# Turning the attention results inside the fourth head's slot, dividing before its last maximum, splitting the maxima on GpSimd, and batch 2's last sum later

## The chip, the cores and the metric

The kernel runs on one core of one Trainium2 chip. The time is that of one execution in device microseconds; the kernel before took 545.0 us, the median of three executions (544.27 to 546.27). TensorE (PE in the rows) multiplies and writes PSUM, which has eight banks of 128x512 float32; VectorE (DVE) and ScalarE (ACT) read PSUM; GpSimd (POOL) works on SBUF only; SyncE (SP) issues DMAs. Each engine runs its own stream in order, and streams wait for one another by semaphores.

## The reference

Four sequences of 512 rows with 128 channels go through two blocks, each with a normalization before and after. `H` is 16 heads.

```python
x = x + layernorm(attention1(layernorm(x)))        # 16 heads of 8, rotary, causal
x = x + layernorm(ffn_block(layernorm(x)))

def attention(...):                                 # both blocks, per head
    scores = q @ k.T * scale                        # 512 x 512
    scores = where(causal, scores, -big)
    attn = softmax(scores)                          # exp(s - max) / sum
    return (attn @ v) @ Wo

def ffn_block(x):
    x = x + attention2(rmsnorm(x, w_ln1))           # 16 heads of 64, keys and values from a latent of 16
    y = rmsnorm(x, w_ln2)
    return x + mean(shared_experts(y)) + sum(top2_gate(y) * experts(y))
```

## The kernel before

**Groups and slots.** The 16 heads of a sequence are taken four at a time. There are 32 such groups (`NG`), 16 of the first block's attention (`LAYER` 1) and then 16 of the second's (`LAYER` 2). The program of every engine is written out slot by slot: in slot n, `stream` runs `main(n, hh)` for the four heads `hh` and behind each head the stages that the table `beside()` puts there (norms, projections, rotations, experts of other sequences). Three groups are in work in one slot:

- group n+2: scores for the row maxima (`scores_for_max`, L574/L576, with the causal mask added by L601), 11 bank fills per slot. VectorE reads each fill and leaves the negated maxima in `NM` (`maximum`, L1263 and L1273). The last fill of a slot, (head 3, i 3), holds the first 128 rows of four heads.
- group n: scores for the exponentials (`scores_for_exp`, L610/L616), ten units per slot; ScalarE's L895 turns each into probabilities in `PG`. The bank of a unit comes free when the exponential three units back is done. The row maximum enters these scores as additional rows of the queries.
- group n-1: GpSimd zeroes what lies above the diagonal in four blocks (L1209 or L1216, semaphore `causal`); TensorE multiplies with the values in four steps j (`values`, L659), all into the one bank `BK_O`; ScalarE copies that bank to `OT` (L901, `ot_ready`); TensorE turns it back into the same bank (`turn_out`, L666, `o_turned`).

**Who waits around the change.** In the kernel before, `turn_out(n-1)` is the last thing of head 3 on TensorE. VectorE divides by the sums (`divide`: reciprocal L1311 into `rec`, product L1320 into `ON1`, or into `ON2`, which the rows call `room`, since it lies in `room1`; semaphore `on_ready`) in the next slot, between the first maxima of head 0. The first `values` step of the next group sits behind head 1's first two units and waits for `on_ready`, for `causal` and for `exp_done`. Probabilities lie in two halves of `PG`.

**The split of the maxima.** The maxima go to TensorE's operands in parts of lower precision: for block 1 three bfloat16 parts (`MB`; four VectorE steps L1293 to L1299), for block 2 two parts (`MF`; two steps L1301 and L1303), each step waiting for the one before (`m_step`). In slot n, VectorE splits group n+1 between the maxima of head 0. TensorE turns the parts at the end of head 1 (`turnmax`, L707/L710), ScalarE copies them to `MP` and SyncE's DMA writes them into the query rows, for slot n+1.

**The end.** Behind the last group, slot 33 holds what is left of sequences 2 and 3. VectorE takes the stages of that list in its order: `o2y` of sequence 3 (sum and variance), `y3` of sequence 2 (L1617, then the statistics), `rms2` of sequence 3 (L1494: tiles 2 and 3 of `xn`; ScalarE scales tiles 0 and 1), then `logit`, the routing and the experts.

Of the kernel before, what the change touches and what calls it, by code (L numbers as in the profile page):

```python
# [16 lines left out]
F32 = mybir.dt.float32  # L17
# [51 lines left out]
def beside():  # L69
# [17 lines left out]
    def experts(b, n, slots):  # L87
# [54 lines left out]
        ("y3", 2, 0), ("rms2", 3, 0), ("x3T", 3, 0), ("logit", 3, 0))]  # L142
# [116 lines left out]
def block_program(nc, x, wqkv, wo1, wkva, wq_nope, wq_rope, wkvb, wo2, ln1w, ln2w, wgate, gbias, wgu, wgu_s, wd,  # L259
                  wd_s, ident, masks, rope1, ropek, ropeq, rank, expert_rows, out):  # L260
    with ExitStack() as ctx:
# [298 lines left out]
        def _(pe):  # L560
# [116 lines left out]
            def main(n, hh):  # L677

                if hh == 0 and n + 2 < NG:
                    m = n + 2  # L680
                    if m == 0:
                        pe.wait_ge(consts_ready, CONSTS)

                if n + 2 == 0 and hh == 2:
                    pe.wait_ge(stack1_late, 32)
                for i in range(4):
                    if 0 <= n < NG and i < 2 + hh % 2:
                        scores_for_exp(n, hh, i)
                    if n + 2 < NG and i < fills_of(hh)[1]:
                        if hh == 0 and i == 0:  # L690
                            stack_loaded(n + 2)
                        scores_for_max(n + 2, hh, i)
                    if 1 <= n <= NG and (hh, i) in VALUES_AT:
                        values(n - 1, VALUES_AT.index((hh, i)))
                if hh == 3 and 1 <= n <= NG:
                    turn_out(n - 1)
# [401 lines left out]
        def _(pool):  # L1098
# [103 lines left out]
            def causal_blocks1(n):  # L1202
# [3 lines left out]
                for j in CAUSAL_ORDER:  # L1206
# [11 lines left out]

            def main(n, hh):
                if hh == 0 and 1 <= n <= NG and LAYER[n - 1] == 1:  # L1220
                    causal_blocks1(n - 1)
                if hh == 2 and 0 <= n < NG and LAYER[n] == 2:
                    causal_blocks2(n)
# [12 lines left out]
        def _(dve):  # L1236
# [45 lines left out]
            def split_max(n, i):  # L1282

                m = NM[:, :, HG * (n % G):HG * (n % G) + HG]
                if i == 0:
                    dve.wait_ge(fill_read, (n + 1) * FILLS)
                    if n:
                        dve.wait_ge(bank_full, BANK0["turnmax", n - 1, 0] + 1)
                elif MSTEPS[n] + i < MSTEPS[n + 1]:
                    dve.wait_ge(m_step, MSTEPS[n] + i)  # L1290
                if LAYER[n] == 1:
                    if i == 0:
                        dve.tensor_copy(MB[:, :, 0, :], m).then_inc(m_step, 1)  # L1293
                    elif i == 1:
                        dve.tensor_tensor(MRest[:], m, MB[:, :, 0, :], ALU.subtract).then_inc(m_step, 1)
                    elif i == 2:
                        dve.tensor_copy(MB[:, :, 1, :], MRest[:]).then_inc(m_step, 1)
                    else:
                        dve.tensor_tensor(MB[:, :, 2, :], MRest[:], MB[:, :, 1, :], ALU.subtract).then_inc(m_step, 1)  # L1299
                elif i == 0:  # L1300
                    dve.tensor_copy(MF[:, :, 0, :], m).then_inc(m_step, 1)  # L1301
                elif i == 1:
                    dve.tensor_tensor(MF[:, :, 1, :], m, MF[:, :, 0, :].bitcast(F32), ALU.subtract).then_inc(m_step, 1)  # L1303
# [20 lines left out]
            def main(n, hh):  # L1324
                split, out = hh == 0 and 0 < n + 1 < NG, hh == 0 and 2 <= n <= NG + 1
                if hh == 0 and n == -1:
                    for i in range(4):
                        split_max(0, i)
                for i in range(4):
                    if split:  # L1330
                        split_max(n + 1, i)
                    if out and i < 2:
                        divide(n - 2, i)
# [371 lines left out]
```

## Time and profile before

| | |
|---|---|
| median of three executions | 545.0 us (544.27 to 546.27) |
| profiled execution, whole time | 546.34 us |
| its span, first to last instruction | 544.6 us |
| mean granted TensorE clock | 0.983 of full speed |
| TensorE matmul busy | 491.0 us, 90% of the span |
| VectorE busy | 401.6 us, 74% |
| ScalarE busy | 312.4 us, 57% |
| GpSimd busy | 200.6 us, 37% |

Durations below come from the one profiled execution. A matmul's row spans its latency, so matmuls in a row overlap. "Idle before" in square brackets is the time in which the engine did nothing ahead of the row, with what ended it; for an instruction that waits for several engines, this name is only an inference. A GpSimd row's span is rough.

### The profile page before, as it was taken

Reading aid. Unit: us, or ns where it says so; the run is one execution under the profiler, and the core shown is the slowest. Engines: PE = TensorE matmul, PEld = TensorE weight load, DVE = VectorE, ACT = ScalarE, POOL = GpSimd, SP = SyncE. Lnnn points to the kernel's source line nnn. Section 1 sums busy time; section 2 is a strip of 40 time slices with the busy share of each in tenths; the row PEclk is TensorE's granted clock in tenths of the full one; section 3 lists DMA queues with packets and bytes.
Section 4 is the critical chain, followed back from the end, with each engine's and each line's share of the span. In section 5 each row is a group of like instructions: output and inputs, shape, how many; then the busy total and the mean of one; then the engine's idle time right before and its main releaser. Section 6 shows DMA issues by size and latency. Waiting matters only on the chain.

```text
span 544.6 us, 9510 instructions
## 1 busy us (share of the span) xinstructions
PE 491.0 (90%) x3190; PEld 281.9 (52%) x3190; DVE 401.6 (74%) x1209; ACT 312.4 (57%) x586; POOL 200.6 (37%) x268
## 2 busy tenths in 40 slices
PE   7788989988799889989999999998989898898784
PEld 3443444434354345556565666564856474554643
DVE  6789998799489977975786687775676854464475
ACT  1586785767667785666756546544465433654230
POOL 5522663365236642664346514521041100510100
PEclk9999999989999999999999999999999998999988
DMA  6455533114223634548345652632303200000000
GB/s 147 132 159 182 159 114 118 45 47 143 82 85 123 172 68 107 107 123 156 117 105 110 125 136 86 135 58 58 59 21 61 58 2 2 20 2 0 2 13 26
DMA packets 29673, 47.17 MB, mean 87 GB/s; under 512 B 4649, under 2 KB 15145, under 8 KB 29113
## 3 DMA queue, kind: packets, MB, share of 16 engines
q1 hardware_dynamic: 28496, 45.72, 32.5%
q10 hardware_dynamic: 1128, 0.85, 0.7%
q8 instruction: 25, 0.41, 0.4%
q14 instruction: 24, 0.19, 0.1%
HBM read 27.22 MB, written 18.87 MB: 85 GB/s over the span
## 4 chain that ended last, share of the span: by engine, by line
PE 58%; DVE 15%; ACT 14%; issue 5%; POOL 4%; DMA 2%; SPq 1%; ACTq 1%; DVEq 0%; POOLq 0%
PE ps L659 14%; PE ps L616 11%; PE ps L729 10%; PE ps L576 5%; DVE ps L1273 4%; ACT PG L895 4%; PE ps L610 4%; PE ps L862 3%; PE ps L574 2%; ACT xn L1034 2%; PE ps L780 2%; PE ps L710 2%; PE ps L601 1%; ACT QS L970 1%; DMA rope_sb<-in_rope 1%
## 5 line engine op out<-in xcount | busy, mean ns | idle before, releaser
L895 ACT ACTIVATE PG<-ps 128x512 f32<-128x512 f32 x320 | 178.5, 600 | 127.6 <-PE ps L616 81.9
L1273 DVE CUSTOM_DVE_ANT_0 ps<-ps,below 128x512 f32<-128x512 f32 (+1 forms) x256 | 156.1, 638 | 40.9 <-PE ps L576 21.8
L616 PE MATMUL ps<-QS,K 128*128 128x512 f32 x320 | 115.8, 446 | 4.8 <-ACT PG L895 3.1
L659 PE MATMUL ps<-PG,V 128*32 128x512 f32 (+3 forms) x1024 | 97.1, 452 | 12.2 <-DVE ON L1320 5.1
L616 PEld LDWEIGHTS ps<-QS,K 128*128 128x128 f32 x320 | 54.0, 190 | 47.7 <-ACT PG L895 21.4
L1263 DVE TENSOR_REDUCE NM<-ps 128x2 f32<-128x512 f32 (+1 forms) x96 | 63.3, 685 | 16.3 <-PE ps L601 16.1
L576 PE MATMUL ps<-K,QS 96*128 96x256 f32 (+3 forms) x256 | 71.4, 336 | 1.1 <-DVEq L1589 0.9
L610 PE MATMUL ps<-QS,KS 128*128 128x128 bf16 (+3 forms) x256 | 62.0, 303 | 5.6 <-ACT PG L895 3.0
L574 PE MATMUL ps<-KS,QS 96*128 96x256 bf16 (+3 forms) x256 | 63.3, 300 | 0.5 <-DVE terms L1379 0.4
L1108 POOL TENSOR_TENSOR rstd<-ve,half 128x4 f32<-128x4 f32 x20 | 20.3, 1017 | 111.8 <-DVE ve L1255 77.9
L1216 POOL TENSOR_SCALAR_AFFINE_SELECT PG<-PG 128x512 f32<-128x512 f32 x64 | 39.7, 643 | 50.0 <-ACT PG L895 49.6
L1209 POOL TENSOR_SCALAR_AFFINE_SELECT PG<-PG 128x512 f32<-128x512 f32 x64 | 38.6, 635 | 41.7 <-ACT PG L895 41.7
L1164 POOL TENSOR_TENSOR whole<-terms 128x512 f32<-128x512 f32 x27 | 34.2, 1277 | 53.3 <-DVE terms L1379 32.4
L576 PEld LDWEIGHTS ps<-K,QS 96*128 96x128 f32 x256 | 44.5, 190 | 10.9 <-DVEq L1589 1.4
L659 PEld LDWEIGHTS ps<-PG,V 128*32 128x32 f32 x1024 | 21.0, 108 | 52.5 <-issue 36.3
L610 PEld LDWEIGHTS ps<-QS,KS 128*128 128x128 bf16 x256 | 19.4, 98 | 49.0 <-ACT PG L895 27.7
L729 PE MATMUL ps<-QS,KS 128*128 128x512 f32 x72 | 35.9, 622 | 0.0
L1273 DVE DVE_READ_ACCUMULATOR2_ANT NM<- 128x1 f32 x256 | 35.8, 140 | 0.0
L601 PE MATMUL ps<-below,identb 128*128 128x256 bf16 (+1 forms) x96 | 30.2, 315 | 0.0
L574 PEld LDWEIGHTS ps<-KS,QS 96*128 96x128 bf16 x256 | 23.2, 97 | 13.2 <-DVE NM L1273 2.8
L1197 POOL TENSOR_TENSOR QC<-whole,QC 128x512 fp32r<-128x512 f32 x16 | 20.5, 1280 | 21.7 <-ACT QC L1017 21.5
L564 PE MATMUL ps<-OT 128*128 128x512 bf16 x76 | 23.7, 424 | 1.5 <-DVE two_ones L1625 1.5
(170 smaller groups left out, 676.5 us busy)
## 6 DMA issues: line engine op xcount, KB each, us to landing
scr<-QC SPq DMA_DIRECT2D x24, 512.0 KB, 2.8
QS<-scr SPq DMA_DIRECT2D x64, 128.0 KB
scr<-room SPq DMA_DIRECT2D x20, 256.0 KB, 2.6
QS<-scr SPq DMA_DIRECT2D x15, 288.0 KB
KS<-scr SPq DMA_DIRECT2D x15, 288.0 KB
QS<-scr SPq DMA_DIRECT2D x64, 64.0 KB
x<-in_x SPq DMA_DIRECT2D x4, 256.0 KB, 3.3
out_x<-x SPq DMA_DIRECT2D x3, 256.0 KB, 2.3
```

Of the source, the lines that this page charges most:

```text
L574: return pe.matmul(dst, QS1[0:MROW, h, P * i:P * i + P], KS1[0:MROW, h, 0:P * k], start=first, stop=alone, skip_group_check=not alone)
L576: return pe.matmul(dst, QS2[0:MROW, h, P * i:P * i + P], K1[0:MROW, SEQ[n] % 2, 0:P * k], start=first, stop=alone, skip_group_check=not alone)
L601: mm = pe.matmul(last, identb[:], below[:, 3 * P:T].unsqueeze(1).to_broadcast([P, heads, P]), start=False, stop=True, skip_group_check=True)
L610: return pe.matmul(dst, KS1[:, h, q0:q0 + P], QS1[:, h, q0:T], start=True, stop=True)
L616: mm = pe.matmul(bank.rearrange("p (h q) -> p h q", h=HG), keys[:, SEQ[n] % 2, P * j:P * j + P], QS2[:, heads, P * i:P * i + P], start=(ke ...
L659: mm = pe.matmul(out, v, p, start=(j == 0), stop=(j == NT - 1), skip_group_check=True)
L729: pe.matmul(bank(u)[0:rows, :], w, xT, start=True, stop=True).then_inc(bank_full, 1)
L895: act.activation(PG[:, n % 2, unit_place(LAYER[n], (u + k) % UNITS), :], ps[:, BANK_OF["unit", u + k], :], ACT.Exp, scale=scale).then_inc( ...
L1209: pool.affine_select(blocks, blocks, pattern=[*heads, [1, P]], compare_op=ALU.is_ge, fill=0.0, base=0, channel_multiplier=-1).then_inc(cau ...
L1216: pool.affine_select(blocks, blocks, pattern=[[0, HG], [1, P]], compare_op=ALU.is_ge, fill=0.0, base=0, channel_multiplier=-1).then_inc(ca ...
L1263: dve.tensor_reduce(dst, src, AX.X, ALU.max, negate=True).then_inc(fill_read, 1)
L1273: dve.tensor_tensor_reduce(out=bank[:, 0:w], in0=bank[:, 0:w], in1=below[:, T - w:T], scale=-1.0, scalar=-NEG, op0=ALU.add, op1=ALU.min, a ...
```

## The change

Four edits:

1. `turn_out(n-1)` is issued in the middle of head 3: behind its second pair (exponential unit and maximum fill, i = 1), ahead of unit i = 2 and the fills i = 2 and 3.
2. `divide(n-1)` moves from head 0 of the next slot to head 3 of the same slot, both instructions together, ahead of the last maximum (i = 3).
3. The splits of groups 1 to 31 move from VectorE to GpSimd, at head 0. In block 1's slots they stand between the second and the third of the four causal blocks; group 0's stays on VectorE. GpSimd's split waits for all maxima of its group (`fill_read`) and for the turn of the previous group's parts.
4. In slot 33's list `rms2` of sequence 3 is ahead of `y3` of sequence 2.

```diff
-        ("y3", 2, 0), ("rms2", 3, 0), ("x3T", 3, 0), ("logit", 3, 0))]
+        ("rms2", 3, 0), ("y3", 2, 0), ("x3T", 3, 0), ("logit", 3, 0))]
...
                     if 1 <= n <= NG and (hh, i) in VALUES_AT:
                         values(n - 1, VALUES_AT.index((hh, i)))
-                if hh == 3 and 1 <= n <= NG:
-                    turn_out(n - 1)
+                    if 1 <= n <= NG and (hh, i) == (3, 1):
+                        turn_out(n - 1)
...
+            def split_max(n):
+                m, done = NM[:, :, HG * (n % G):HG * (n % G) + HG], MSTEPS[n]
+                pool.wait_ge(fill_read, (n + 1) * FILLS)
+                pool.wait_ge(bank_full, BANK0["turnmax", n - 1, 0] + 1)
+                if LAYER[n] == 1:
+                    pool.tensor_copy(MB[:, :, 0, :], m).then_inc(m_step, 1)
+                    pool.wait_ge(m_step, done + 1)
+                    pool.tensor_tensor(MRest[:], m, MB[:, :, 0, :], ALU.subtract).then_inc(m_step, 1)
...
+                masked1 = hh == 0 and 1 <= n <= NG and LAYER[n - 1] == 1
+                if masked1:
+                    causal_blocks1(n - 1, CAUSAL_ORDER[:2])
+                if hh == 0 and n >= 0 and n + 1 < NG:
+                    split_max(n + 1)
+                if masked1:
+                    causal_blocks1(n - 1, CAUSAL_ORDER[2:])
...
-                split, out = hh == 0 and 0 < n + 1 < NG, hh == 0 and 2 <= n <= NG + 1
+                out = hh == 3 and 1 <= n <= NG
                 if hh == 0 and n == -1:
-                    for i in range(4):
-                        split_max(0, i)
+                    split_max0()
                 for i in range(4):
-                    if split:
-                        split_max(n + 1, i)
-                    if out and i < 2:
-                        divide(n - 2, i)
+                    if out and i == 3:
+                        divide(n - 1, 0)
+                        divide(n - 1, 1)
                     if n + 2 < NG and i < 2 + hh % 2 + hh // 3:
                         maximum(n + 2, hh, i)
```

TensorE, the end of a slot of block 1 before: L610 is the third exponential unit of head 3, L574 with L601 the two last fills, L666 the turn of the results.

```order
L574 MATMUL ps<-KS,QS 128x384 [waits fill_read]
L610 MATMUL ps<-QS,KS 128x256 [waits exp_done]
L610 MATMUL ps<-QS,KS 128x256
L574 MATMUL ps<-KS,QS 128x256 [waits fill_read]
L574 MATMUL ps<-KS,QS 128x256
L601 MATMUL ps<-below,identb 128x2x128
L574 MATMUL ps<-KS,QS 128x128 [waits fill_read]
L574 MATMUL ps<-KS,QS 128x128 x3
L601 MATMUL ps<-below,identb 128x512
L666 MATMUL ps<-ident_sb,OT 128x128 [waits ot_ready]
L666 MATMUL ps<-ident_sb,OT 128x128 x3
```

The same place now:

```order
L574 MATMUL ps<-KS,QS 128x384 [waits fill_read]
L666 MATMUL ps<-ident_sb,OT 128x128 [waits ot_ready]
L666 MATMUL ps<-ident_sb,OT 128x128 x3
L610 MATMUL ps<-QS,KS 128x256 [waits exp_done]
L610 MATMUL ps<-QS,KS 128x256
L574 MATMUL ps<-KS,QS 128x256 [waits fill_read]
L574 MATMUL ps<-KS,QS 128x256
L601 MATMUL ps<-below,identb 128x2x128
L574 MATMUL ps<-KS,QS 128x128 [waits fill_read]
L574 MATMUL ps<-KS,QS 128x128 x3
L601 MATMUL ps<-below,identb 128x512
```

The four matmuls of the turn, with their wait for ScalarE's copy, have moved ahead of ten others.

VectorE from the two last fills of a slot on, before (L1263 reads a fill of several heads, L1273 one head's, L1311 and L1320 divide):

```order
L1263 TENSOR_REDUCE NM<-ps 128x2 [waits score_fill]
L1263 TENSOR_REDUCE NM<-ps 128x4 [waits score_fill]
L1293 CAST MB<-NM 128x4x4 [waits bank_full,fill_read]
L1311 RECIPROCAL rec<-ps 128x16 [waits o_turned]
L1273 ISA ps,NM<-ps,below 128x512 [waits score_fill]
L1273 ISA NM 128x1
L1295 TENSOR_TENSOR MRest<-NM,MB 128x16 [waits m_step]
L1320 TENSOR_TENSOR ON<-ps,rec 128x4x32 [waits rec_ready]
L1273 ISA ps,NM<-ps,below 128x384 [waits score_fill]
```

The same place now (the lines are numbered anew: L1286 and L1296 are the maxima, L1323 and L1332 the division):

```order
L1286 TENSOR_REDUCE NM<-ps 128x2 [waits score_fill]
L1323 RECIPROCAL rec<-ps 128x16 [waits o_turned]
L1332 TENSOR_TENSOR ON<-ps,rec 128x4x32 [waits rec_ready]
L1286 TENSOR_REDUCE NM<-ps 128x4 [waits score_fill]
L1296 ISA ps,NM<-ps,below 128x512 [waits score_fill]
L1296 ISA NM 128x1
L1296 ISA ps,NM<-ps,below 128x384 [waits score_fill]
```

The division stands one fill earlier than it did, and no split is left in the row. On GpSimd, four causal blocks of a slot stood in a row before:

```order
L1209 AFFINE_SELECT PG<-PG 128x4x128 [waits exp_done,cleared]
L1209 AFFINE_SELECT PG<-PG 128x4x128 x3
L1164 TENSOR_TENSOR whole<-terms 128x512 [waits terms_ready] x2
```

Now the split (L1225 to L1231) is among them:

```order
L1209 AFFINE_SELECT PG<-PG 128x4x128 [waits exp_done,cleared]
L1209 AFFINE_SELECT PG<-PG 128x4x128
L1225 CAST MB<-NM 128x4x4 [waits bank_full,fill_read]
L1227 TENSOR_TENSOR MRest<-NM,MB 128x16 [waits m_step]
L1229 CAST MB<-MRest 128x4x4 [waits m_step]
L1231 TENSOR_TENSOR MB<-MRest,MB 128x4x4 [waits m_step]
L1209 AFFINE_SELECT PG<-PG 128x4x128 [waits exp_done]
L1209 AFFINE_SELECT PG<-PG 128x4x128
```

The third and fourth blocks, and what GpSimd has behind them, come after the split's four steps.

## Rows read from the trace of the kernel before

**Rows 1.** Waits of PE: engine, line, released by: us in total, times, longest us
```profile
PE ps L659 <- DVE ON L1320: 5.1, 5, 1.3
PE ps L659 <- DVE room L1320: 4.6, 4, 1.9
PE ps L724 <- ACT PG L895: 3.4, 4, 1.0
...
PE ps L610 <- ACT PG L895: 3.0, 6, 0.9
...
PE ps L659 <- ACT PG L895: 1.4, 3, 0.5
...
PE ps L659 <- POOL PG L1216: 1.1, 2, 0.8
```

**Rows 2.** Timeline of PE, end of one slot of block 1: start us, us
```profile
78.49 0.38 PE L610 MATMUL ps<-QS,KS 128*128 128x256 bf16 x2
...
79.49 0.60 PE L666 MATMUL ps<-ident_sb,OT 128*128 128x128 f32 x4
...
82.56 1.07 PE L659 MATMUL ps<-PG,V 128*32 128x512 f32 x8 [1.22 <-DVE ON L1320]
```

**Rows 3.** Timeline of DVE, one split step at the slot's start
```profile
70.28 0.88 DVE L1293 CAST MB<-NM 128x16 bf16<-128x16 f32 x1
```

**Rows 4.** Timeline of POOL, the same time and one slot later
```profile
68.86 2.27 POOL L1174 TENSOR_TENSOR terms<-whole,room 128x512 f32<-128x512 f32 x2 [3.03 <-ACT room L935]
71.08 2.41 POOL L1209 TENSOR_SCALAR_AFFINE_SELECT PG<-PG 128x512 f32<-128x512 f32 x4
...
80.36 2.41 POOL L1209 TENSOR_SCALAR_AFFINE_SELECT PG<-PG 128x512 f32<-128x512 f32 x4 [4.41 <-ACT PG L895]
```

**Rows 5.** Timeline of ACT, the copy ahead of the turn, in block 1 and block 2
```profile
78.22 0.60 ACT L901 ACTIVATE OT<-ps 128x512 f32<-128x512 f32 x1
...
346.96 0.60 ACT L901 ACTIVATE OT<-ps 128x512 f32<-128x512 f32 x1
```

**Rows 6.** Timeline of PE, the third unit of head 3 in block 2
```profile
348.55 0.63 PE L616 MATMUL ps<-QS,K 128*128 128x512 f32 x2
```

**Rows 7.** Groups of POOL by form: busy us, mean ns of one
```profile
L1108 POOL TENSOR_TENSOR rstd<-ve,half 128x4 f32<-128x4 f32 x20 | 20.3, 1017 | 111.8 <-DVE ve L1255 77.9 <-DVE ve L1521 22.1 <-DVE ve L1529 11.4
...
L1118 POOL TENSOR_TENSOR nmean<-nmean,rstd 128x4 f32<-128x4 f32 x16 | 3.2, 199 | 1.3
```

**Rows 8.** Groups of DVE by form: first and last of the six split steps
```profile
L1293 DVE CAST MB<-NM 128x16 bf16<-128x16 f32 x16 | 6.3, 394 | 0.5
...
L1301 DVE CAST MF<-NM 128x16 fp32r<-128x16 f32 x16 | 4.7, 296 | 0.8 <-DVE QS L1602 0.2 <-DVE CT L1569 0.2
```

**Rows 9.** Timeline of PE, a turn of the maxima's parts
```profile
76.06 0.39 PE L707 MATMUL ps<-identb,MB 128*12 128x128 bf16 x4
```

**Rows 10.** Window: us; PE, PEld, DVE, ACT, POOL busy; granted clock; DMA; GB/s
```profile
116.60:120.00 3.40, 3.35 (x15) 0.71 (x19) 3.30 (x14) 1.22 (x3) 3.14 (x4) 0.50 0.07 17
```

**Rows 11.** Timeline of PE where the clock falls, and in slot 32
```profile
116.65 1.94 PE L659 MATMUL ps<-PG,V 128*32 128x512 f32 x8 [1.26 <-DVE ON L1320]
...
454.56 1.93 PE L659 MATMUL ps<-PG,V 128*32 128x512 f32 x8 [1.85 <-DVE room L1320]
...
500.96 2.14 PE L659 MATMUL ps<-PG,V 128*32 128x512 f32 x24 [1.87 <-DVE room L1320]
```

**Rows 12.** Timeline of DVE in slot 33
```profile
513.17 0.69 DVE L1617 TENSOR_TENSOR KS<-room,ps 128x512 f32<-128x512 f32 x1 [0.88 <-PE ps L862]
...
515.37 0.47 DVE L1494 TENSOR_SCALAR xn<-KS,rstd 128x128 f32<-128x128 f32 x2
519.25 0.19 DVE L1537 TENSOR_TENSOR KS<-ps,gbias_sb 128x32 f32<-128x32 f32 x1 [3.42 <-PE ps L825]
```

**Rows 13.** Timeline of POOL, then of PE, in slot 33
```profile
512.38 1.01 POOL L1108 TENSOR_TENSOR rstd<-ve,half 128x4 f32<-128x4 f32 x1 [22.12 <-DVE ve L1521]
...
515.89 0.67 PE L724 MATMUL ps<-ident_sb,xn 128*128 128x128 f32 x2 [1.24 <-DVE xn L1494]
```

More of the change, by code:

```diff
@@ L1200, in ropeB, with causal_blocks1 @@
                 pool.sem_inc(job_done[j], 1)
-            def causal_blocks1(n):
+            def causal_blocks1(n, order):
                 pair = PG[:, n % 2, 0:8, :].rearrange("p (h k) t -> p h k t", k=2)
@@ L1205, in causal_blocks1 @@
                 pool.wait_ge(exp_done, UNITS * (n + 1))
-                for j in CAUSAL_ORDER:
+                for j in order:
                     blocks = (pair[:, :, 0, 0:P], pair[:, :, 1, 0:P], both[:, :, :, 0:P], pair[:, :, 1, 3 * P:T])[j]
@@ L1217, in causal_blocks2 @@
                                        channel_multiplier=-1).then_inc(causal, 1)
-            def main(n, hh):
-                if hh == 0 and 1 <= n <= NG and LAYER[n - 1] == 1:
-                    causal_blocks1(n - 1)
+            def split_max(n):
[6 more added lines that the diff above has]
+                    pool.tensor_tensor(MRest[:], m, MB[:, :, 0, :], ALU.subtract).then_inc(m_step, 1)
+                    pool.wait_ge(m_step, done + 2)
+                    pool.tensor_copy(MB[:, :, 1, :], MRest[:]).then_inc(m_step, 1)
+                    pool.wait_ge(m_step, done + 3)
+                    pool.tensor_tensor(MB[:, :, 2, :], MRest[:], MB[:, :, 1, :], ALU.subtract).then_inc(m_step, 1)
+                else:
+                    pool.tensor_copy(MF[:, :, 0, :], m).then_inc(m_step, 1)
+                    pool.wait_ge(m_step, done + 1)
+                    pool.tensor_tensor(MF[:, :, 1, :], m, MF[:, :, 0, :].bitcast(F32), ALU.subtract).then_inc(m_step, 1)
+            def main(n, hh):
+                masked1 = hh == 0 and 1 <= n <= NG and LAYER[n - 1] == 1
[5 more added lines that the diff above has]
+                    causal_blocks1(n - 1, CAUSAL_ORDER[2:])
                 if hh == 2 and 0 <= n < NG and LAYER[n] == 2:
@@ L1280, in maximum, with split_max0 @@
                 reduce_fill(n, k, src, dst)
[L1282 to L1303, printed above, removed]
+            def split_max0():
+                m = NM[:, :, 0:HG]
+                dve.wait_ge(fill_read, FILLS)
+                dve.tensor_copy(MB[:, :, 0, :], m).then_inc(m_step, 1)
+                dve.wait_ge(m_step, 1)
+                dve.tensor_tensor(MRest[:], m, MB[:, :, 0, :], ALU.subtract).then_inc(m_step, 1)
+                dve.wait_ge(m_step, 2)
+                dve.tensor_copy(MB[:, :, 1, :], MRest[:]).then_inc(m_step, 1)
+                dve.wait_ge(m_step, 3)
+                dve.tensor_tensor(MB[:, :, 2, :], MRest[:], MB[:, :, 1, :], ALU.subtract).then_inc(m_step, 1)
             def divide(n, i):
```

## The prediction
> **What bounds the kernel.** I read first who waits for whom on each engine, then the timelines of single slots, then the windows with the granted clock. TensorE is the engine to follow: its matmuls cover nine tenths of the span, and ScalarE and GpSimd idle often. So a change is worth what it takes from TensorE's waits or adds to them. The longest of these in the middle of the program stand ahead of the first values step of a slot, for VectorE's division: 5.1 us in five places and 4.6 us in four, 9.7 us together [rows 1]. The other large one is for an exponential bank at a slot's end (3.4 us ahead of L724, 3.0 ahead of L610) [rows 1]; the change doesn't address that.
>
> **The division (edits 1 and 2).** In the slot shown, the turn L666 ran at 79.49 us and the next values step started at 82.56, after 1.22 us of waiting [rows 2]: in between VectorE had two maxima to finish, a split step, another maximum, and only then the product. Now both instructions come right behind the turn and ahead of a maximum, at least one maximum before the old place, and the values step lies some ten matmuls behind the turn. I take it that no values step waits for the division any more. What is late next is the first causal block. In the slot shown GpSimd starts its four at 80.36 and needs 2.41 us for all [rows 4], a quarter of it is 0.60, so the first is done at 80.96, before TensorE comes. In the slot ahead, GpSimd is held up by L1174 and starts them at 71.08 [rows 4]; the first is done at 71.68, while TensorE's preceding matmul ends about 71.4. There 0.3 us of the wait stays. I count two such slots: 9.7 - 0.6 = 9.1 us. Five more waits ahead of L659 carry another name, 1.4 us in three places (ScalarE) and 1.1 in two (GpSimd) [rows 1]; in most of them the division was in fact the last to end, and I count 1.0 us of the 2.5. Sum: 10.1 us less. Bounds: 9.7 + 2.5 = 12.2 at most, and 1.9 at least (the wait of slot 32 alone, 1.87 us [rows 11], where no exponentials follow that could take its place).
>
> **The turn's own wait (edit 1).** The turn waits for ScalarE's copy. In block 1 that copy ends at 78.22 + 0.60 = 78.82 [rows 5], and TensorE reaches the new place, where L610 starts now, at 78.49 [rows 2]: it will stand 0.33 us, with some 0.06 us for the signal 0.4. The copy follows the exponential of head 2, which itself follows TensorE, so this distance repeats from slot to slot; I find it at 0.33 to 0.43 us in thirteen of block 1's sixteen slots. In eight of these TensorE waits right behind the turn for ScalarE anyway (the waits of L610 and L724 in [rows 1]), and standing earlier costs nothing there. Five are left: 5 x 0.4 = 2.0 us, and 0.3 for a slot or two more. In block 2 the copy ends at 346.96 + 0.60 = 347.56 and TensorE arrives at 348.55 [rows 5, 6], 1 us later: no wait. Cost 2.3 us; bounds 0 and 14 x 0.4 = 5.6. On ScalarE the third exponential of head 3 comes after two others of 0.6 us each behind the copy, which is about the time that the turn takes on TensorE, so it is not late. VectorE's last maximum comes 0.6 us later, but the next slot starts without the split.
>
> **The split (edit 3).** The six step groups of VectorE took 33.0 us in all (6.3 the first and 4.7 the last listed [rows 8]), all but the first group's go. The mean of 394 ns hides two kinds: 0.17 us when alone, 0.88 us at 70.28 [rows 3], ending with GpSimd's L1174 at 71.13 [rows 4]. VectorE isn't the bound, so I value the 32 us at nothing beyond the division's earlier place; bounds 0 and 2 us less (waits of TensorE for routing and rotations, which VectorE's other work delays).
>
> What it costs is four steps in GpSimd's row between causal blocks 2 and 3. The trace has none of this shape there; between 199 ns for a product of 128x4 and 1017 ns for a power of 128x4 [rows 7], I take 0.2 us and 0.07 for each step's signal, nearest to the product, since copies and subtractions are like it: 4 x 0.27 = 1.1 us in block 1, 0.5 in block 2. In the slot shown the split then runs 81.6 to 82.7 and the third block ends at 83.3; its values step comes 2.9 us behind the first, near 84.2 even when this starts 1.2 us sooner. The turn of the parts is later still: at 76.06 [rows 9] in a slot whose split would end at 73.4. So both are covered by 0.9 us and more, and in block 2, where the causal blocks aren't behind the split, by over 2 us. Value nothing; bounds 0 and the rival below.
>
> The Trainium skill (SBUF — State Buffer, "SBUF: two separate sides") says that VectorE and GpSimd share a port pair as an exclusive lock, taken by a GpSimd instruction or by a VectorE one with two SBUF inputs; the trace agrees with the 0.88 us step. By this rule the four steps can in turn be held by such a VectorE instruction, some 0.7 us each time, which would use up most of the cover but not change the sum. The skill (GPSIMD Engine Reference, "Engine selection") advises VectorE for elementwise work and gives GpSimd about half the speed with two inputs. At 0.17 us here that would be 0.35 a step, 1.6 us for four, still under the cover; no row here shows this shape.
>
> **The clock.** From 116.60 to 120.00 the granted clock is 0.50, TensorE's lower level of 1.2 GHz, while PE is busy 3.35 of 3.40 us [rows 10]; the same holds from 454.5 to 457.9. Both begin within 0.1 us of the end of a long wait for the division, 1.26 and 1.85 us [rows 11], and the eight matmuls there took 1.94 and 1.93 instead of 1.07 us [rows 2, 11]. Other waits of 1.2 us didn't lower it, so this is no law. If those two go, each gives back 0.9 us for the matmuls and some 0.3 for the next: 2.4 us less. Bounds: 3.4 less (half of both windows), and 3.4 more if as much low clock appears elsewhere.
>
> **The end (edit 4).** VectorE runs L1617 from 513.17 with its statistics until L1494 can start at 515.37 [rows 12]; the scale that L1494 needs is there from 512.38 + 1.01 = 513.39 on [rows 13]. Moved ahead it ends near 514.0, and TensorE's second pair of turns, which waited 1.24 us for it [rows 13], follows the first without a wait. Gain 1.2 us. The 2.2 us of L1617 and statistics then lie from 514.0 to 516.3, ahead of L1537, which would start near 518.0 (519.25 less 1.2) [rows 12]; GpSimd's scale and the store of sequence 2 have 20 us left. Bounds 0.8 and 1.3.
>
> **Sum.** 10.1 + 1.2 + 2.4 less, 2.3 more: 11.4 us. I let 0.9 go in one slot in which ScalarE waits for a chain over GpSimd (the norm of sequence 1 or 0) and not for TensorE: 10.5 us. The profiled execution took 546.34 us with a span of 544.6; it becomes 535.8 with a span of 534.1. The median shown is 1.3 us below that execution, so the forecast is 545.0 - 10.5 = 534.5 us. What a measurement tells from no change is 0.5%, 2.7 us.
>
> **Rivals.**
> *The turn's wait is paid in full.* If the slots lose their bank wait once TensorE runs sooner, all fourteen pay 0.4 us, 5.6 in all, and stretches of low clock stay: 10.1 + 1.2 - 5.6 = 5.7 less, 539.3 us. For it speaks the constancy of the 0.33 us; against it that the bank waits come from ScalarE's own work in those slots.
> *The clock falls elsewhere.* Four new stretches like [rows 10] cost 1.7 us each, 6.8, and the two old ones stay in part: 545.0 - 10.5 + 6.8 = 541.3 us. For it: a wait of 0.4 us in many slots; against it, most waits of over 1 us get shorter.
> *ScalarE takes over.* The bank waits [rows 1] grow by what the division's waits lose; only slot 32 and the end stay gained (1.9 + 1.2), less a part of the turn's wait: 543.0 us. Against it: ScalarE idles 0.6 us and more several times in each slot.
> *GpSimd's split holds the values.* If a step takes as long as the power, 1.1 us with its signal, the third causal block ends at 81.6 + 4.4 + 0.6 = 86.6, 2.4 us after its values step is due. In some fourteen slots of block 1 that is 34 us, less the 10.5: 568 us. It decides from a step of about 0.5 us on, and at 0.7 the cost (0.8 us x 14 = 11) already turns the result to slower than before. For it: no row of this shape, and rough spans on GpSimd; against it the 199 ns.
>
> **Chances and range.** Forecast 0.60, the turn's wait 0.18, the clock 0.07, ScalarE 0.08, GpSimd 0.07. The first three are faster by over 0.5%, 0.85; ScalarE's within 0.5%, 0.08; the last slower, 0.07. The forecast alone spans 531 to 538. The range reaches to the second and third cases, and for more clock and cover down to 530: 530.0 to 541.5 us, which leaves out about 0.2.
>
> **What would show it.** In the profile after: no wait of PE L659 for ON or room, and at most 0.4 us for GpSimd's blocks; PE waits ahead of L666 for ACT OT of 0.3 to 0.4 us in block 1, under 6 us in sum, and none in block 2; the split's steps on POOL about 0.2 us each; VectorE's busy time down by over 30 us; no clock of 0.50 near the two old places; L724's second pair in slot 33 without a wait. It is wrong if PE waits for POOL PG ahead of the third or fourth values step, if the waits for ACT PG grow by more than 3 us, or if the low clock adds up to over 7 us in the middle.

## The result and the profile after

The changed kernel took 537.98 us, the median of four executions (535.69 to 538.62); the kernel before took 544.94 beside it. The ratio is 0.9862 [0.9827, 0.9896]: 7.0 us less, or 1.3%, where the forecast was 10.5. Measured again (experiment e5) it took 536.01 us, ratio 0.9835 [0.9805, 0.9864]. Over all ten executions the median is 536.6 us, 8.4 us less than before. Medians and ratios leave out disturbed executions (three are on record, of 575, 678 and 1614 us). The profiled execution took 538.62 us with a span of 535.6.

First the waits of TensorE after (engine, line, released by: us in total, times, longest), then from the page the group of the values steps (busy us, mean ns of one, idle before).

```profile
PE ps L666 <- ACT OT L901: 4.5, 14, 0.7
PE ps L729 <- DVE CT L1579: 4.1, 3, 1.8
PE ps L616 <- ACT PG L895: 3.1, 2, 1.6
PE ps L724 <- ACT PG L895: 2.3, 4, 1.0
...
PE ps L610 <- ACT PG L895: 2.0, 4, 1.1
```
```profile
L659 PE MATMUL ps<-PG,V 128*32 128x512 f32 (+3 forms) x1024 | 95.5, 446 | 1.2 <-POOL PG L1209 0.7 <-POOL PG L1216 0.3
```

The 9.7 us of waits for ON and room in [rows 1] are gone, and 1.0 us for GpSimd's blocks is what L659 still waits. The turn L666 now waits 4.5 us. Of its 14 waits one, 0.7 us in slot 32, has ScalarE's last copy as its cause and isn't from the change, so 3.8 us in 13 places are new. The exponential banks' waits (L724, L610) fell from 6.4 us to 4.3.

The end of the slot of [rows 2] after: PE, then ACT, POOL and the division on DVE (start us, us).

```profile
78.94 0.66 PE L666 MATMUL ps<-ident_sb,OT 128*128 128x128 f32 x4 [0.22 <-ACT OT L901]
...
79.44 0.38 PE L610 MATMUL ps<-QS,KS 128*128 128x256 bf16 x2
...
81.78 1.07 PE L659 MATMUL ps<-PG,V 128*32 128x512 f32 x8
```
```profile
78.29 0.60 ACT L901 ACTIVATE OT<-ps 128x512 f32<-128x512 f32 x1
...
80.53 1.23 POOL L1209 TENSOR_SCALAR_AFFINE_SELECT PG<-PG 128x512 f32<-128x512 f32 x2 [2.58 <-ACT PG L895]
80.80 0.25 DVE L1323 RECIPROCAL rec<-ps 128x16 f32<-128x16 f32 x1
...
81.08 0.29 DVE L1332 TENSOR_TENSOR ON<-ps,rec 128x128 f32<-128x128 f32 x1
...
82.03 0.20 POOL L1225 CAST MB<-NM 128x16 bf16<-128x16 f32 x1 [0.28 <-DVE NM L1286]
...
82.31 0.22 POOL L1227 TENSOR_TENSOR MRest<-NM,MB 128x16 f32<-128x16 f32 x1
...
82.60 0.20 POOL L1229 CAST MB<-MRest 128x16 bf16<-128x16 f32 x1
...
82.88 0.22 POOL L1231 TENSOR_TENSOR MB<-MRest,MB 128x16 bf16<-128x16 f32 x1
...
83.05 1.22 POOL L1209 TENSOR_SCALAR_AFFINE_SELECT PG<-PG 128x512 f32<-128x512 f32 x2
```

The turn waits 0.22 us for a copy that ends at 78.89. The product ends at 81.37, and L659 starts at 81.78 without a wait. GpSimd's split runs from 82.03 to 83.1 in steps of 0.20 to 0.22 us.

Slot 33 after, DVE and PE, against [rows 12, 13]:

```profile
506.75 0.48 DVE L1504 TENSOR_SCALAR xn<-KS,rstd 128x128 f32<-128x128 f32 x2 [1.18 <-POOLq L1116]
507.15 0.68 DVE L1627 TENSOR_TENSOR KS<-room,ps 128x512 f32<-128x512 f32 x1
...
510.02 0.19 DVE L1547 TENSOR_TENSOR KS<-ps,gbias_sb 128x32 f32<-128x32 f32 x1 [0.60 <-PE ps L825]
```
```profile
507.50 0.66 PE L724 MATMUL ps<-ident_sb,xn 128*128 128x128 f32 x4 [1.17 <-ACT xn L1034]
```

All four turns L724 are one row now: the second pair no longer waits.

**Three parts of the span.** I cut each profile at two marks, the first values step of the first group and that of the last (500.96 in [rows 11] for the kernel before). The windows of the kernel before, then after, then three low ones of after (us; PE, PEld, DVE, ACT, POOL busy; granted clock; DMA share; GB/s):

```profile
50.12:500.96 450.84, 419.06 (x2799) 240.28 (x2799) 337.85 (x1018) 275.32 (x532) 175.41 (x240) 0.99 0.34 86
500.96:544.60 43.64, 30.44 (x179) 20.66 (x179) 24.27 (x80) 9.26 (x19) 4.69 (x6) 0.87 0.05 13
```
```profile
51.10:494.22 443.12, 420.01 (x2780) 241.23 (x2797) 318.94 (x928) 276.69 (x532) 192.75 (x328) 0.99 0.35 88
494.22:535.64 41.42, 29.04 (x180) 19.54 (x179) 25.48 (x82) 9.27 (x19) 4.70 (x6) 0.90 0.05 13
...
138.60:142.00 3.40, 3.40 (x5) 1.34 (x5) 0.69 (x1) 1.58 (x3) 0.01 (x1) 0.50 0.00 0
241.00:244.40 3.40, 3.40 (x15) 1.71 (x13) 2.76 (x14) 1.72 (x3) 2.10 (x4) 0.50 0.57 177
367.20:370.70 3.50, 3.50 (x9) 2.49 (x8) 2.07 (x5) 1.19 (x2) 1.22 (x2) 0.51 0.72 129
```

The time of the profiled executions, 546.34 and 538.62, differs by -7.7 us: +1.0 ahead of the first mark, -7.7 in the middle, -2.2 in the tail and +1.2 outside the span (1.7 and 3.0 us). The first mark varies by itself (50.1, 51.0 and 51.7 in three profiles of kernels whose start is the same), and it goes with low clock at the start: the two profiles without a stretch at 0.50 near 12 us, the first of the kernel before and e8's, have it at 50.1 and 50.0, ten others with such a stretch at 51.0 to 52.4. So the 1.0 us isn't put down to the change. The middle holds three stretches at a granted clock of 0.50 (1.2 GHz) after, two before, and none of the three is where the two were.

### The profile page after: what moved, and what is told of

Same layout as the page of the kernel before. It is cut to its first block, busy times and chain, and to the rows that moved or that the text cites. A ratio compares the mean times of both kernels' runs of the same rounds, so it can differ in the third digit from the quotient of the medians.

```text
span 535.6 us, 9488 instructions
## 1 busy us (share of the span) xinstructions
PE 491.0 (92%) x3168; PEld 282.4 (53%) x3190; DVE 383.9 (72%) x1117; ACT 313.7 (59%) x586; POOL 218.8 (41%) x360
## 4 chain that ended last, share of the span: by engine, by line
PE 64%; ACT 15%; POOL 8%; DVE 6%; issue 4%; DMA 1%; ACTq 1%; DVEq 0%; POOLq 0%; SPq 0%
PE ps L659 14%; PE ps L729 13%; PE ps L616 12%; PE ps L576 6%; ACT PG L895 4%; PE ps L610 4%; PE ps L862 3%; PE ps L574 3%; ACT xn L1034 2%; PE ps L666 2%; POOL rstd L1108 2%; PE ps L780 2%; PE ps L601 2%; PE ps L710 2%; POOL terms L1174 1%
## 5 line engine op out<-in xcount | busy, mean ns | idle before, releaser
L1296 DVE CUSTOM_DVE_ANT_0 ps<-ps,below 128x512 f32<-128x512 f32 (+1 forms) x256 | 155.7, 646 | 40.8 <-PE ps L576 20.3
L616 PE MATMUL ps<-QS,K 128*128 128x512 f32 x320 | 119.2, 456 | 4.4 <-ACT PG L895 3.1
L659 PE MATMUL ps<-PG,V 128*32 128x512 f32 (+3 forms) x1024 | 95.5, 446 | 1.2 <-POOL PG L1209 0.7
L1286 DVE TENSOR_REDUCE NM<-ps 128x2 f32<-128x512 f32 (+1 forms) x96 | 65.7, 687 | 26.9 <-PE ps L601 26.7
L616 PEld LDWEIGHTS ps<-QS,K 128*128 128x128 f32 x320 | 54.1, 192 | 46.2 <-ACT PG L895 23.1
L574 PE MATMUL ps<-KS,QS 96*128 96x256 bf16 (+3 forms) x256 | 63.0, 299 | 1.7 <-issue 0.6
L610 PE MATMUL ps<-QS,KS 128*128 128x384 bf16 (+3 forms) x237 | 54.4, 295 | 4.6 <-ACT PG L895 2.0
L576 PEld LDWEIGHTS ps<-K,QS 96*128 96x128 f32 x256 | 45.0, 192 | 10.5 <-DVEq L1599 0.9
L610 PEld LDWEIGHTS ps<-QS,KS 128*128 128x128 bf16 x256 | 20.1, 98 | 45.6 <-ACT PG L895 25.8
L659 PEld LDWEIGHTS ps<-PG,V 128*32 128x32 f32 x1024 | 20.4, 108 | 41.5 <-issue 31.2
L1296 DVE DVE_READ_ACCUMULATOR2_ANT NM<- 128x1 f32 x256 | 36.3, 142 | 0.0
L729 PE MATMUL ps<-QS,KS 128*128 128x512 f32 x72 | 36.2, 628 | 0.0
L601 PE MATMUL ps<-below,identb 128*128 128x256 bf16 (+1 forms) x96 | 30.2, 315 | 0.0
L574 PEld LDWEIGHTS ps<-KS,QS 96*128 96x128 bf16 x256 | 23.5, 97 | 11.6 <-DVE NM L1296 1.9
L666 PE MATMUL ps<-ident_sb,OT 128*128 128x128 f32 x128 | 20.0, 279 | 4.6 <-ACT OT L901 4.5
```

What stands on the lines that cost most here:

```text
L574: return pe.matmul(dst, QS1[0:MROW, h, P * i:P * i + P], KS1[0:MROW, h, 0:P * k], start=first, stop=alone, skip_group_check=not alone)
L576: return pe.matmul(dst, QS2[0:MROW, h, P * i:P * i + P], K1[0:MROW, SEQ[n] % 2, 0:P * k], start=first, stop=alone, skip_group_check=not alone)
L601: mm = pe.matmul(last, identb[:], below[:, 3 * P:T].unsqueeze(1).to_broadcast([P, heads, P]), start=False, stop=True, skip_group_check=True)
L610: return pe.matmul(dst, KS1[:, h, q0:q0 + P], QS1[:, h, q0:T], start=True, stop=True)
L616: mm = pe.matmul(bank.rearrange("p (h q) -> p h q", h=HG), keys[:, SEQ[n] % 2, P * j:P * j + P], QS2[:, heads, P * i:P * i + P], start=(ke ...
L659: mm = pe.matmul(out, v, p, start=(j == 0), stop=(j == NT - 1), skip_group_check=True)
```

## The experiments

The table collects what the profiles showed: the length of the middle, the low-clock stretches of 3.4 us in it, and the middle with 1.45 us taken off for each. That figure is from the same kernels profiled twice: before with two (450.8) and with none (448.0, e6), after with three (443.1) and with none (438.75, e5), that is 1.4 and 1.46 each. Slot by slot these five stretches cost 1.1 to 1.7 us, so a middle corrected this way is uncertain by some 0.3 us per stretch.

| kernel | turn behind | divide | split on | middle | low | without | tail | median us | ratio |
|---|---|---|---|---|---|---|---|---|---|
| before | head's end | next slot | DVE | 450.8 | 2 | 447.9 | 43.6 | 545.0 | 1 |
| e6 = before | | | | 448.0 | 0 | 448.0 | 43.7 | 546.4 | 1.0013 |
| e7 | head's end | next slot | DVE | 449.6 | 1 | 448.1 | 41.5 | 544.3 | 0.9970 |
| after | pair 2 | same slot | POOL | 443.1 | 3 | 438.8 | 41.4 | 538.0 | 0.9862 |
| e5 = after | | | | 438.75 | 0 | 438.75 | 42.9 | 536.0 | 0.9835 |
| e1 | pair 2 | same slot | DVE | 441.1 | 0 | 441.1 | 42.8 | 538.9 | 0.9882 |
| e2 | head's end | next slot | POOL | 443.8 | 1 | 442.4 | 43.8 | 539.6 | 0.9889 |
| e3 | pair 3 | same slot | POOL | 436.2 | 0 | 436.2 | 41.7 | 531.1 | 0.9735 |
| e4 | head's end | same slot | POOL | 436.4 | 0 | 436.4 | 41.9 | 532.0 | 0.9748 |
| e9 | pair 3 | same slot | DVE | 436.2 | 0 | 436.2 | 42.9 | 533.8 | 0.9784 |
| e8 | pair 2, copy early | same slot | POOL | 438.6 | 1 | 437.1 | 44.4 | 533.6 | 0.9788 |
| e11 | pair 3 | same slot | POOL, long | 448.7 | 2 | 445.8 | 41.5 | 543.7 | 0.9953 |

**e1: the turn and the division alone.** The kernel before with edits 1 and 2; the split stays on VectorE.

```diff
-                if hh == 3 and 1 <= n <= NG:
-                    turn_out(n - 1)
+                    if 1 <= n <= NG and (hh, i) == (3, 1):
+                        turn_out(n - 1)
...
-                    if out and i < 2:
-                        divide(n - 2, i)
+                    if out and i == 3:
+                        divide(n - 1, 0)
+                        divide(n - 1, 1)
```

> Edits 1 and 2 alone: the split stays on VectorE, the end's order as before. Theory A (the gain is the division's waits, whoever splits): TensorE's waits for ON and room ahead of L659 vanish (9.7 us before), the turn costs 4 to 5 us of waiting for OT, and of the 7.0 us gained by all four edits about 4 to 6 remain: 539 to 541 us. Theory B (what helps is that VectorE is rid of the split, held up by GpSimd's port use): without edit 3 nothing is gained, the turn's wait is only paid: 545 to 548 us.

538.9 us, ratio 0.9882 [0.9852, 0.9912]. All waits for ON and room are gone, so they go by edits 1 and 2 alone. The middle is 6.9 us shorter than in e6, 2.35 us less than with the split on GpSimd too (e5). Where such time goes, one slot shows: POOL, DVE and PE of e1, then DVE and PE of e5, at the same place.

```profile
165.47 2.43 POOL L1209 TENSOR_SCALAR_AFFINE_SELECT PG<-PG 128x512 f32<-128x512 f32 x4 [0.19 <-ACT PG L895]
...
167.26 0.66 DVE L1295 TENSOR_TENSOR MRest<-NM,MB 128x16 f32<-128x16 f32 x1
...
168.05 1.06 PE L659 MATMUL ps<-PG,V 128*32 128x512 f32 x8
...
168.52 0.17 DVE L1299 TENSOR_TENSOR MB<-MRest,MB 128x16 bf16<-128x16 f32 x1
168.61 2.48 DVE L1380 TENSOR_TENSOR terms<-ps,ropeq_sb 128x512 f32<-128x512 f32 x4
...
171.15 0.39 PE L574 MATMUL ps<-KS,QS 96*128 96x256 bf16 x2 [0.44 <-DVE terms L1380]
```
```profile
166.47 2.48 DVE L1389 TENSOR_TENSOR terms<-ps,ropeq_sb 128x512 f32<-128x512 f32 x4
...
166.98 1.06 PE L659 MATMUL ps<-PG,V 128*32 128x512 f32 x8
...
169.48 0.38 PE L574 MATMUL ps<-KS,QS 96*128 96x256 bf16 x2
```

In e1 one split step takes 0.66 us: it ends at 167.92, with GpSimd's blocks at 167.90. The steps stand ahead of the rotation's products L1380, and TensorE waits 0.44 us for these ahead of the next fill. The products start 0.56 us after the first values step in e1, and 0.51 us ahead of it in e5. This slot is 0.61 us longer in e1. Four slots between 155 and 217 us make 1.7 of the 2.35 together; the wait for the rotation's products is seen in two of them, and what lengthens the other two wasn't followed up.

The largest single part stands in the stretch that begins with the values step at 125.5 us (126.1 in e5), 1.34 us longer in e1. There ScalarE's scaling L1034 waits for a norm's last factor, which GpSimd works out from VectorE's statistics; in e1 the split stands ahead of these statistics on VectorE. The row of e1, then that of e5:

```profile
133.36 1.65 ACT L1034 ACTIVATE xn<-x,nmean_xn,rstd_xn 128x128 f32<-128x128 f32 x4 [1.70 <-POOL nmean_xn L1138]
```
```profile
132.63 1.65 ACT L1034 ACTIVATE xn<-x,nmean_xn,rstd_xn 128x128 f32<-128x128 f32 x4 [0.36 <-POOL nmean_xn L1138]
```

One stretch goes the other way. From 115.6 us on, the slot is 0.71 us longer in e5 than in e1, because GpSimd has its split ahead of the same kind of chain, and ScalarE waits for that chain in e5 and not in e1:

```profile
122.28 1.65 ACT L1034 ACTIVATE y_b<-y_b,nmean,rstd 128x128 f32<-128x128 f32 x4 [0.59 <-POOL nmean L1118]
```

**e2: the split alone.** The kernel after with the old turn, the old division and the old order at the end.

> Edit 3 alone: the split on GpSimd, turn, division and end as before. Theory A: without the split's steps between, the division comes 0.3 us sooner in block 2 and 0.7 to 1.3 sooner in block 1, so some 4 of the 9.7 us of waits for ON and room go, with no wait for OT at the turn: 541 to 543 us. Theory B: nearly all of the change's gain: 538 us.

539.63 us, ratio 0.9889 [0.9862, 0.9915], nearly as much as e1. Its waits ahead of L659 for VectorE:

```profile
PE ps L659 <- DVE room L1332: 4.2, 4, 1.9
...
PE ps L659 <- DVE ON L1332: 0.6, 1, 0.6
```

Of the five waits for ON (5.1 us) one of 0.6 us is left although the division stands where it did: with no split step between maximum and product, the product is nearly in time. In three of the other places TensorE now waits 0.3 to 0.4 us for ScalarE (1.0 us in all). The four long ones of block 2 stay. So edit 3 takes the same waits in block 1 as edits 1 and 2, and the parts don't add: -6.9 and -5.6 alone, -9.3 together.

**e3: the turn one pair later.** The kernel after with

```diff
-                    if 1 <= n <= NG and (hh, i) == (3, 1):
+                    if 1 <= n <= NG and (hh, i) == (3, 2):
```

> All four edits, but the turn stands behind the pair i = 2 of head 3 and not i = 1 (one exponential unit and one fill later, some 0.6 us of TensorE). If the 4.5 us of waits of L666 for OT are a loss, they fall under 0.5 us while L659's waits stay near 1 us, and the time is 2 to 4 us below the changed kernel: 534 to 536 us. If ScalarE's bank waits behind the turn take it all back, it equals the changed kernel: 538 us.

531.14 us, ratio 0.9735 [0.9708, 0.9762]: the best version, 5 to 7 us below the changed kernel's medians. Windows and waits of e3, then the windows of e5:

```profile
51.48:487.69 436.21, 414.20 (x2799) 239.43 (x2798) 317.76 (x928) 275.63 (x532) 193.08 (x328) 1.00 0.35 89
487.69:529.43 41.74, 30.72 (x180) 20.58 (x179) 25.45 (x82) 9.27 (x19) 4.72 (x6) 0.88 0.05 13
```
```profile
PE ps L724 <- ACT PG L895: 3.8, 4, 1.0
PE ps L610 <- ACT PG L895: 3.7, 6, 1.6
...
PE ps L666 <- ACT OT L901: 0.7, 1, 0.7
```
```profile
51.68:490.43 438.75, 416.65 (x2799) 238.96 (x2798) 318.39 (x928) 276.72 (x532) 193.23 (x328) 1.00 0.35 89
490.43:533.37 42.94, 30.73 (x180) 19.98 (x179) 25.46 (x82) 9.27 (x19) 4.71 (x6) 0.89 0.05 13
```

Without low clock in either middle, the turn's early place costs 438.75 - 436.21 = 2.5 us. From values step to values step, seven slots are longer in e5: by 0.44, 0.43, 0.41, 0.14 and 0.51 us in block 1 and by 0.26 twice in block 2, 2.45 of the 2.5. In the others the wait of 0.2 to 0.4 us only takes the place of one for a bank: L724 and L610 wait 7.5 us here and 4.3 with the early turn. The tail is 1.2 us shorter than e5's although its program is the same (the wait L729 <- DVE CT near 26 us in the tail is 0.7 in place of 1.85). The medians differ by more than the profiles do; that rest isn't settled.

**e4: the turn where it was, the division behind the slot's last maximum.**

```diff
-                    if 1 <= n <= NG and (hh, i) == (3, 1):
-                        turn_out(n - 1)
+                if hh == 3 and 1 <= n <= NG:
+                    turn_out(n - 1)
...
+                if out:
+                    divide(n - 1, 0)
+                    divide(n - 1, 1)
```

> All four edits, but the turn stands where it was before (end of head 3) and the division right behind the last maximum of the same slot. No wait of L666 for OT; the division is done about 0.7 us later than in the changed kernel. If that is soon enough for L659 (waits for ON and room under 2 us), the time is 535 to 537 us; if VectorE's last maximum pushes it past the values step, the waits come back with some 4 us: 538 to 541 us.

531.95 us, ratio 0.9748 [0.9723, 0.9774], its middle within 0.2 us of e3's, and no wait for ON or room. The turn needn't be early at all. What mattered is that the division isn't behind the next slot's first maxima: e2 and e4 both have the split on GpSimd and the turn at the head's end, and with the division in the same slot the middle is 6.0 us shorter (442.4 against 436.4).

**e5: the changed kernel again.**

> The changed kernel once more, unaltered, as a second profile and for its spread. The stretches of low clock: in its first profile three lie in the middle (from 138.6, 241.0 and 367.2 us) and these slots are 1.1 to 1.9 us longer for it. If the clock falls by chance at other places from one execution to the next, this profile has them elsewhere, or more or fewer, and its span differs from 535.6 by about 1.5 us for each; if the turn's wait for OT itself lowers the clock at these places, they are there again.

536.01 us. The turn's waits are the same to the tenth (4.5 us, 14 places), but the low clock of the middle is gone: its window above has a granted clock of 1.00. PE of after and then of e5 at the place where the first stretch of after begins:

```profile
138.37 1.93 PE L729 MATMUL ps<-xT,wabs_sb 128*128 128x512 f32 x2 [1.74 <-ACT xT L924]
```
```profile
139.00 1.12 PE L729 MATMUL ps<-xT,wabs_sb 128*128 128x512 f32 x2 [1.74 <-ACT xT L924]
```

One and the same wait of 1.74 us, with the lower level behind it in one execution and not in the other.

**e6: the kernel before again.**

> The kernel before once more, unaltered. Two things are looked for: whether its low clock is again at 116.6 and 454.5 us, behind the long waits for the division (then the waits cause it), and whether the first exponential of slot 0 starts at 43.4 us as in its first profile or near 44.5 to 45.0 as in all five of the changed ones (then that 1 us is the start's own scatter and no effect of the change). Time 544.3 to 546.3 us.

546.42 us, ratio 1.0013 [0.9995, 1.0030]. The waits for ON and room are those of [rows 1]; the values step of [rows 11] at 116.65 and the window behind its wait in e6:

```profile
117.62 1.06 PE L659 MATMUL ps<-PG,V 128*32 128x512 f32 x8 [1.27 <-DVE ON L1320]
```
```profile
117.50:120.90 3.40, 3.28 (x32) 1.21 (x33) 3.30 (x14) 1.87 (x4) 3.22 (x4) 1.00 0.13 34
```

The same wait, and the clock stays at full speed: the eight matmuls take 1.06 us and not 1.94. So neither the division's waits in the kernel before nor the turn's after decide by themselves where the low clock falls; it differs between executions of one kernel.

**e7: the end alone.** The kernel before with `("rms2", 3, 0)` ahead of `("y3", 2, 0)`.

> Edit 4 alone: rms2 of sequence 3 ahead of y3 of sequence 2, all else as before. The prediction's term: 1.2 us less (0.8 to 1.3), 543.7 us, if nothing else in the end waits. Rival: another wait takes its place there (ScalarE's copy of xT3 or the logits), and it is 0 to 0.5 us less, or 1.9 less if the end's stretch of low clock gets shorter too, as the changed profiles suggest.

544.33 us, ratio 0.997 [0.9954, 0.9986]: 1.6 us less [0.8, 2.5]. Its tail in the profile is 2.2 us shorter, with 2.5 us less of low clock in it. The tails of e6 and e5 differ by 0.8, but their low clock isn't equal either (11.5 and 9.7 us). Alike are the tails with one stretch of 3.4 us and one at the very end: 42.8 us with the old order (e1), 41.4 to 41.5 with the new one (after, e7, e11), 1.3 to 1.4 less.

In the middle e7 has one low stretch, at 455.2 us, behind the wait of 1.86 us for the division, where the first profile of the kernel before had one too and e6 none. A link between such a wait and a fall is thus neither shown nor excluded. Counted over all profiles it changes nothing: the four profiles with the division's waits (before, e6, e7, e2) have 2, 0, 1 and 1 stretches, the eight without them 3, 0, 0, 0, 0, 0, 1 and 2.

**e8: ScalarE's copy earlier.** The kernel after with the copy `OT` ahead of the second exponential of head 2.

```diff
                         if hh == 2 and k == 1:
+                            copy_out(n)
```

> The changed kernel with the turn left behind i = 1, but ScalarE copies to OT ahead of the second exponential of head 2 and not behind it, so the copy ends about 0.5 us sooner. If the wait of L666 for OT is what the turn's early place costs, it falls from 4.5 us to under 1 and the time comes near that of the turn behind i = 2 (531.1 us): 531 to 533.5. If it is the place itself (the third exponential unit of head 3 comes late for ScalarE or the fills for VectorE), the time stays at 537 to 538 us.

533.64 us, ratio 0.9788 [0.9766, 0.981]. The middle is 1.6 us shorter than in e5 once its one low stretch is taken off: no slot's turn waits before the last, but L616 waits once for the query rows' DMA (1.3 us, 0.9 in e5).

**e9: e3 with the split on VectorE.** Edit 3 undone in e3.

> As the turn behind i = 2 (531.1 us), but the split is back on VectorE (edit 3 undone; edit 4 kept). Theory A: with the division ahead of the last maximum nobody waits for the split's steps, so 531 to 532.5 us. Theory B: relieving VectorE is worth 2 us and more by itself (waits for routing, rotations and fills): 533 to 536 us.

533.79 us, ratio 0.9784 [0.9754, 0.9814]. Its middle:

```profile
51.30:487.52 436.22, 414.86 (x2798) 239.06 (x2798) 335.83 (x1016) 275.31 (x532) 175.13 (x240) 1.00 0.36 89
```

436.22 against 436.21 us in e3: with the turn in its better place the split on GpSimd brings nothing in the middle, and VectorE's 18 us more of work cost nothing in sum. Slot by slot the two aren't equal: e3 loses 0.71 us in the stretch from about 115 us on, as e5 does, and 0.4 in another, and wins 0.1 to 0.5 in four, so the zero is a balance. The medians still differ by 2.6 us, 1.2 of it in the two profiles' tails; why is open.

**e10 and e11: long steps on GpSimd.** e3 with eight more copies of 128x16 in GpSimd's split in block 1.

```diff
+                    for k in range(8):
+                        step(pool.tensor_copy(spare[:], MRest[:]))
```

> As the turn behind i = 2, but GpSimd's split in block 1 has eight more copies of 128x16 in its row, about 0.27 us each, 2.2 us in all, as if each of its four steps took 0.8 us. It prices the rival that the split holds the values. By the cover that the prediction gave (0.9 us and more ahead of the third values step): 1.3 us too late in some fourteen slots, 18 us slower, 549 us, with waits of L659 for POOL PG. If the cover is larger than 2.2 us: 531 us still.

543.45 us, ratio 0.9959 [0.9937, 0.9982]: 12.3 us above e3. The profile is from the same kernel run once more:

> The kernel of e10 once more, for its profile (that of e10 fell on a disturbed execution). By the theory that GpSimd's split holds the values once its steps are long, PE waits ahead of L659 for GpSimd's blocks in most of block 1's slots, about 12 us in sum beside 1 us with the short steps, and the span is 12 to 13 us above that with the short ones (529.4). If the time went elsewhere (the turn of the parts L707, the query rows), the waits ahead of L659 stay under 4 us and others grow.

543.69 us, ratio 0.9953 [0.9926, 0.9979]. Waits of PE, then one slot, POOL and PE:

```profile
PE ps L660 <- POOL PG L1210: 8.0, 8, 1.3
```
```profile
85.95 2.00 POOL L1231 COPY spare<-MRest 128x16 f32<-128x16 f32 x8
...
88.46 1.22 POOL L1210 TENSOR_SCALAR_AFFINE_SELECT PG<-PG 128x512 f32<-128x512 f32 x2
89.16 0.64 PE L660 MATMUL ps<-PG,V 128*32 128x256 f32 x8 [1.05 <-POOL PG L1210]
```

Eight copies take 2.00 us and the third values step then waits 1.05 us for its block, so 0.95 us of the delay were covered in this slot, as the prediction had it (0.9 and more). Waits for GpSimd's blocks stand in 8 places, 8.0 us together beside 0.7 in e3. Two of them, of 0.35 us, are those that e3 has; the six long ones (1.05 to 1.3 us) stand in six of 15 slots, and in the others the 2 us were covered. The middle is 9.6 us longer, so 2.3 us came in other ways that weren't followed up. Rival four is real. Where it bites, the cover is what was worked out; it bites in six slots and not in fourteen, which is why e10 cost 12.3 us and not 18.

## Why the prediction was right, and where it was off

The predicted 534.5 us lies 3.5 below the first median and 1.5 below the second; both are inside the range, and the direction and mechanism held. The terms, against the profiles without low clock in the middle (e6, e5) and e3, e9:

- **The division, 10.1 less (9.2 with what was let go).** The waits went as said: none for ON or room, 1.0 us for GpSimd's blocks, in three places of at most 0.4. By itself, from e6 to e9, it is 448.0 - 436.2 = 11.8 us, near the upper bound of 12.2. The 0.9 that was let go for a chain over GpSimd and ScalarE is real where GpSimd splits: the stretch from 115.6 us on is 0.71 longer in e5 than in e1 and in e3 than in e9.
- **The turn's own wait, 2.3 more.** With the split on GpSimd 2.5 us (e5 against e3), with five slots of block 1 that pay 1.9 together, as counted (2.0); 13 new waits of 0.2 to 0.4, mostly 0.22 where 0.4 was put. New are two slots of block 2 at 0.26 each; the turn doesn't wait there, as expected, so this came in another way that wasn't followed up. With the split on VectorE it is twice as much, 441.1 - 436.2 = 4.9 us (e1 against e9), a coupling that no term had.
- **The split, nothing (bounds 0 and 2 less).** This value was mis-sized: 2.35 us less beside the early turn (e1 against e5), and nothing beside the late one (e3 against e9). Both are balances of slots that win and of one that loses 0.71. VectorE isn't the bound on average, but with the early turn its row decides when the rotation's products, the next fills and a norm's statistics come. The costs were right: steps of 0.20 to 0.22 us, covered ahead of the values steps. The half speed that the Trainium skill gives GpSimd (GPSIMD Engine Reference, "Engine selection") doesn't fit at this size: 220 ns for the 128x16 difference against 170 on VectorE, 1.3 times as long, and a product with a quarter of the elements takes 199 [rows 7]. The lock of the Trainium skill (SBUF — State Buffer, "SBUF: two separate sides") agrees with the 0.66 us step of e1, a VectorE one with two SBUF inputs that ended with GpSimd's blocks. The 0.88 us step of [rows 3], on which the prediction rested it, is a cast with one input, so it's no instance of two inputs; why it was long isn't shown. The other direction, GpSimd's steps held by VectorE, no run showed: the four groups of block 1 have means of 197 to 221 ns.
- **The clock, 2.4 less: this step failed.** It rested on two stretches that began right behind the division's waits [rows 10, 11]. e6 has the waits without the stretches, and the changed kernel has had three and none. Nor did the executions as a whole gain clock: the mean granted clock is 0.986 over the changed kernel's ten and 0.985 over 58 of the kernel before. What I read as a consequence was, as far as these runs tell, the scatter of single executions; the term should have been 0 with a range of some 1.5 us per stretch either way. It is about the size of the difference from the measurement: without it the sum is 8.1 less, against 8.4 over all ten executions.
- **The end, 1.2 less.** 1.6 by e7's ratio [0.8, 2.5], 1.3 to 1.4 by tails with like low clock (e1 against after, e7, e11), and L724's second pair doesn't wait any more. The step holds, and its size too.
- **Outside the span, not priced.** Time less span is 1.7 us on average for before, e6, e7 and 1.8 for e1, and 2.2 to 2.7 for the kernels with the split on GpSimd (2.4 after; e9, with VectorE's split, has 2.0). That is 0.4 to 0.9 us more; no run tested why.

At equal clock the middle is 9.3 shorter (-11.8 + 4.9 - 2.35), the tail 1.3, and 0.65 is lost outside: some 10 against the 8.1 of the forecast without its clock term. Over ten executions 8.4 were measured; the 1.6 between isn't accounted for, and sums from single profiles are no more exact than that. That the forecast of 10.5 came near is in part luck: it had 2.4 us of clock that didn't come and too little for division and split.

Two of the signs named failed. The low clock in the middle came to 10.2 us in the first profile after (three stretches), over the 7 us that were to show the forecast wrong, and to nothing in the second; the rival with low clock elsewhere happened in the one execution and not in the other. And VectorE's busy time fell by 17.7 us, not by over 30 (401.6 to 383.9). The 33.0 us were row times that overlap their neighbours; without the six groups VectorE's busy time in the kernel before is only 21.4 us less. The rival in which the turn's wait is paid in full lost as a description (most waits were absorbed), though its 539.3 us lies nearer the first median than the forecast does; ScalarE as the new bound would have shown in L724 and L610, which wait less than before.

## What to carry to other kernels

When a wait for a result is to go, move the instruction that produces it ahead of unrelated work on its own engine first (in e4, beside the split's move and the end's order, that alone takes the middle from 442.4 to 436.4 us); issuing the turn on the other engine earlier too bought only a wait for what feeds the turn. A difference between a low clock's place in two single profiles is no evidence of a cause: profile the same kernel twice before the clock gets a term in a sum. Price edits that touch the same wait together, since their gains don't add. When work moves to another engine, look at what it now stands ahead of there: GpSimd's split delayed a norm's chain by 0.7 us in one slot, and long steps held the values in six.

## What the runs showed of the hardware

- Low clock in the middle came in pieces of 3.4 us, zero to three per execution of one and the same kernel, at 1.4 to 1.5 us each on average (1.1 to 1.7 slot by slot). The waits that such stretches followed were there without them in other executions (e5, e6).
- A VectorE step of 128x16 takes 0.17 us in many rows, and 0.66 (e1) and 0.88 us (before) in two that end with a long GpSimd instruction; the same step on GpSimd takes 0.20 to 0.22, and its group's mean hardly moves (eight copies in a row: 197 ns each, 0.25 us from start to start).
- An engine can have a quarter of its time free and still set a slot's length by the order in its row: 2.35 us in the middle from 18 us of small steps, or none in sum, depending on where TensorE's turn stood (e1 against e5, e9 against e3).
